# Causal attention scored with keys on partitions: row maxima from a rough first pass, no transposes of probabilities

## What is computed

```python
qkv = xn @ W_qkv                                  # 128 -> 2048 + 1024 + 1024
bias = slope[h] * (pos_k - pos_q)
scores = where(causal, q @ k.T / sqrt(64) + bias, -inf)
s = (softmax(scores) @ v).reshape(B, S, 2048) @ W_out
h = gelu(xn @ w1[e] + b1[e]); y = h @ w2[e] + b2[e]   # per expert e
ffn = sum over the 2 best experts of softmax weight * y
out = x + s * silu(ffn)
```

## Time and profile before

| | |
|---|---|
| Runs | 1374.01, 1370.53, 1371.32 us |
| Span of the profiled execution, first to last instruction | 1341.2 us |
| Profiled execution's own time | not listed; the median run is 30.1 us over the span |
| PE busy | 1257.6 us (94%) |
| DVE busy | 1237.7 us (92%) |
| ACT busy | 1082.2 us (81%) |
| POOL busy | 845.9 us (63%) |
| Mean granted TensorE clock | 0.984 of full speed |

### The profile page before, as it was taken

How to read it: one execution, slowest core, us unless ns; L and a number is a source line. 1 busy time by engine, 2 the same in 40 slices (tenths; PEclk the granted TensorE clock), 3 DMA queues, 4 the chain that set the end, 5 groups by cost and what they waited for, 6 DMA issues and landing times.

```text
span 1341.2 us, 56170 instructions
## 1 busy us (share of the span) xinstructions
PE 1257.6 (94%) x17434; PEld 1072.9 (80%) x17435; DVE 1237.7 (92%) x3788; ACT 1082.2 (81%) x2175; POOL 845.9 (63%) x993
## 2 busy tenths in 40 slices
PE   2599999999999999998999899999999999999993
PEld 1387888888888888886888678888888888888882
DVE  8798999999999999996888799999999999999996
ACT  1488998899889888885666688888888888888883
POOL 6277777777777777772000177777777777767774
PEclk9699999999999999999999999999999999999997
DMA  8132333323333333331222222222222222222222
GB/s 314 38 76 68 78 78 75 74 72 78 76 76 75 78 78 78 78 76 31 84 81 81 79 70 70 70 67 65 68 67 68 70 70 70 65 65 69 67 71 63
DMA packets 96213, 103.28 MB, mean 77 GB/s; under 512 B 17170, under 2 KB 76594, under 8 KB 95540
## 3 DMA queue, kind: packets, MB, share of 16 engines
q1 hardware_dynamic: 92084, 94.46, 27.5%
q0 software_dynamic: 4096, 8.40, 2.2%
HBM read 18.91 MB, written 16.78 MB: 27 GB/s over the span
## 4 chain that ended last, share of the span: by engine, by line
PE 89%; DVE 5%; issue 3%; ACT 1%; POOL 1%; DMA 1%; SPq 0%; ACTq 0%; DVEq 0%; POOLq 0%
PE ps L643 20%; PE ps L634 10%; PE ps L635 10%; PE ps L567 9%; PE ps L569 9%; PE ps L568 9%; PE ps L665 6%; PE ps L666 5%; PE ps L667 5%; PE ps L676 4%; PE ps L733 1%; DVE mix L945 1%; POOL h L547 1%; DMA X<-in_L_attn_inputs 1%; ACT stage L850 1%
## 5 line engine op out<-in xcount | busy, mean ns | idle before, releaser
L547 POOL TENSOR_TENSOR h<-stage 128x512 f16<-128x512 f32 x640 | 663.4, 1045 | 193.8 <-ACT stage L265 106.7
L850 ACT ACTIVATE stage<-stage,nmax 128x256 f32<-128x256 f32 (+3 forms) x1024 | 530.1, 564 | 17.4 <-DVE nmax L998 11.7
L998 DVE CUSTOM_DVE_ANT_0 stage<-ps,relpos,nslope_now 128x256 f32<-128x256 f32 (+3 forms) x1024 | 522.5, 543 | 12.8 <-PE ps L635 8.3
L643 PE MATMUL ps<-ident,stage 128*128 128x128 f32 x2560 | 389.8, 275 | 4.4 <-ACT stage L850 4.3
L265 ACT COPY stage<-ps 128x512 f32<-128x512 f32 x512 | 299.6, 586 | 89.4 <-PE ps L643 82.4
L643 PEld LDWEIGHTS ps<-ident,stage 128*128 128x128 f32 x2560 | 300.4, 141 | 63.8 <-ACT stage L850 19.5
L635 PE MATMUL ps<-k_st,q_st 128*128 128x256 f16 (+3 forms) x1024 | 299.5, 300 | 0.0
L634 PE MATMUL ps<-k_st,q_st 128*128 128x256 f16 (+3 forms) x1024 | 272.3, 299 | 12.8 <-DVE nmax L998 6.4
L665 PE MATMUL ps<-v_sp,stage 128*128 128x65 f16 x2560 | 265.6, 194 | 0.9 <-POOL h L547 0.9
L666 PE MATMUL ps<-v_sp,stage 128*128 128x64 f16 x2560 | 265.8, 193 | 0.0
L667 PE MATMUL ps<-v_sp,h 128*128 128x65 f16 x2560 | 264.7, 192 | 0.0
(11 more groups left out here) (170 smaller groups left out, 2604.2 us busy)
## 6 DMA issues: line engine op xcount, KB each, us to landing
q_st<-q_raw SPq DMA_DIRECT2D x512, 64.0 KB
k_st<-k_raw SPq DMA_DIRECT2D x256, 128.0 KB, 2.4
xg<-slot_x SPq DMA_DIRECT2D x40, 128.0 KB, 2.0
slot_y<-y_sb SPq DMA_DIRECT2D x40, 128.0 KB, 1.7
slot_x<-att SPq DMA_DIRECT2D x2, 2048.0 KB, 13.3
wx_raw<-in_L_ffn_w SPq DMA_DIRECT2D x64, 64.0 KB, 1.9
X<-in_L_attn_inputs SPq DMA_DIRECT2D x4, 512.0 KB, 5.7
stage<-in_L_attn_W_qkv SPq DMA_DIRECT2D x2, 1024.0 KB, 6.9
```

The source lines that it names most:

```text
L547: pool.tensor_tensor(t_lo[r], t_p[r], upper(t_p[r]), ALU.subtract).then_inc(s[f"lo{u % NG}"], 1)
L643: mm = pe.transpose(T_ps[u % 2][:, b * P:(b + 1) * P], prob[u % 2][:, b * P:(b + 1) * P], ident[:, :])
L850: e = act.activation(prob[u % 2][:, c0:c0 + w], neg_s[u % 2][:, c0:c0 + w], ACT.Exp, bias=nmax[:, u % 2, k:k + 1], scale=-1.0)
L998: ins = dve.tensor_tensor_reduce(neg_s[u % 2][:, c0:c0 + w], S_ps[u % 2][:, c0:c0 + w], relpos[:, SEQ - w:SEQ], nslope_now[:, sl, h:h + 1] ...
```

## The change

**Scores are computed transposed.** Keys stand on partitions, and queries in the free dimension. `GROUPS` is now cut by key tile kt (128 keys, the (4-kt)·128 queries that see them), again eight pieces in five groups. Exp then yields probabilities that already have keys on partitions, so T and X are gone, with `ON_ACT`, `neg_s`, `prob` and the two transposing banks.

**Bias and shift enter through the contraction.** `k_st` and `q_st` have two planes. Plane 0 is 128 rows deep (hi and lo of q against hi of k, twice). Plane 1 is 67 rows deep (`EXTRA`): hi of q against lo of k, the key position (row 64), and the shift of each query (row 65 holds c/1024 against 1024), with a last row for the query tile. A third matmul of 128 columns per piece (`ident16` against `maskT`) adds the causal mask to the diagonal block. Exp reads PSUM directly, with the head's slope as scale.

**Row maxima come from a rough pass.** M (`rough`): for each slot and head, hi of q (64 rows deep) against hi of k, queries on partitions, in three rounds per slot (`ROUNDS`) over two PSUM banks, one per head; head 0 uses partitions 0 to 63, head 1 64 to 127. B (`peaks`, DVE) replaces R: the same custom instruction with `kmask` in place of `relpos`, max in place of min, its full output thrown away (`junk`). C (`turn_shifts`, PE) transposes the 8 columns of maxima of a slot; ACT (`shifts`) makes 16-bit rows of them, and two small DMAs on SP (`place_shifts`) put them in row 65 of `q_st`. M and B of a body run one window ahead of its scores.

**The rest.** N handles both heads of a slot in one reciprocal and one product (two per body in place of four). The copies of the slopes (L1010) are gone. K and Q of slot 0 run two windows ahead; `k_st` and `v_sp` have two buffers, so the loop body is written out twice (`UNROLL`). The index copies on POOL (I) stand apart from the indirect DMAs (D) that need them. `go_ahead` starts each half with K, Q and V of its first body; six windows of a half are straight code ahead of the loop (two of them entering) and three behind it. POOL fills the constant rows once at the start.

```diff
-GROUPS = [[(0, 3, 0)], [(0, 0, 0), (0, 2, 128)], [(0, 1, 0), (1, 1, 256)], [(1, 3, 0)],
-          [(1, 0, 0), (1, 2, 128)]]
+GROUPS = [[(0, 0, 0)], [(0, 1, 0), (0, 3, 384)], [(0, 2, 0), (1, 2, 256)], [(1, 0, 0)],
+          [(1, 1, 0), (1, 3, 384)]]
+ROUNDS = [[(3, 0)], [(0, 0), (2, 128)], [(1, 0)]]
...
-        ("S0", 0), ("T9", -1), ("A0", -1), ("S1", 0), ("P5", -1), ("P7", -1), ("P6", -1),
+        ("S1", 0), ("C1", 0), ("P8", -1), ("P9", -1), ("S2", 0), ("M0", 1), ("A0", -1), ("S3", 0), ("A1", -1),
...
+            def rough(n, par, j):
+                sl, r = divmod(j, NR)
+                need(pe, f"qh{sl}", n + 1)
+                need(pe, f"kst{sl}", (n + 1) * 32)
+                if r == 0:
+                    need(pe, f"crow{1 - sl}", n + sl)
+                else:
+                    need(pe, f"peak{j - 1}", n + 1)
...
+                for i, c0 in ROUNDS[r]:
+                    w = (i + 1) * P
+                    for h in range(2):
+                        head = slice(DH * h, DH * h + DH)
+                        mm = pe.matmul(M_ps[h][:, c0:c0 + w], q_raw[sl][head, 0, i * P:(i + 1) * P],
+                                       k_st[par][sl][head, 0, 0:w], start=True, stop=True)
+                mm.then_inc(s[f"rough{j}"], 1)
+            def turn_shifts(n, _, sl):
+                for r in range(NR):
+                    need(pe, f"peak{sl * NR + r}", n + 1)
+                pe.transpose(M_ps[0][:, 0:P], mx[sl][:, :], ident[:, :]).then_inc(s[f"turnc{sl}"], 1)
...
-                group_done(pe, "shifted", n, u - 2)
...
+                need(pe, f"cst{sl}", (n + 1) * 32)
+                group_done(pe, "exp", n, u - 2)
...
+                for h, kt, c0 in GROUPS[u % NG]:
+                    d = S_ps[u % 2][:, c0:c0 + (QT - kt) * P]
+                    at, seen = slice(kt * P, (kt + 1) * P), slice(kt * P, SEQ)
+                    pe.matmul(d, k_st[par][sl][:, 0, at], q_st[sl][h][:, 0, seen], start=True, stop=False)
+                    pe.matmul(d, k_st[par][sl][0:EXTRA, 1, at], q_st[sl][h][0:EXTRA, 1, seen],
+                              start=False, stop=False)
+                    mm = pe.matmul(d[:, 0:P], ident16[:, :], maskT[:, :], start=False, stop=True)
...
-            def turn(n, u):
-                group_done(pe, "exp", n, u)
-                group_done(pe, "out", n, u - 2)
-                for b in range(4):
-                    mm = pe.transpose(T_ps[u % 2][:, b * P:(b + 1) * P],
-                                      prob[u % 2][:, b * P:(b + 1) * P], ident[:, :])
-                mm.then_inc(s[f"turned{u % NG}"], 1)
...
+            def shifts(n, _, sl):
+                act.wait_ge(s[f"turnc{sl}"], n + 1)
+                need(act, f"cst{sl}", n * 32)
+                act.activation(c16[sl][:, :], M_ps[0][0:2 * QT, 0:P], ACT.Copy, scale=-1.0 / 1024)\
+                   .then_inc(s[f"crow{sl}"], 1)
...
+                parts = [(0, 0, 256), (1, 256, 512)] if r == 2 else [(GROUPS[r][0][0], 0, 512)]
+                for h, c0, c1 in parts:
+                    e = act.activation(t_p[r][:, c0:c1], S_ps[u % 2][:, c0:c1], ACT.Exp,
+                                       scale=slope[:, bass.ds(pair_index(n) * 2 * SLOTS + sl * 2 + h, 1)])
...
+                for h in range(2):
+                    for i, c0 in ROUNDS[r]:
+                        w = (i + 1) * P
+                        ins = dve.tensor_tensor_reduce(
+                            junk[h][:, c0:c0 + w], M_ps[h][:, c0:c0 + w], kmask[:, SEQ - w:SEQ], 1.0, -3e38,
+                            ALU.add, ALU.max, mx[sl][:, h * QT + i:h * QT + i + 1])
...
+                for h in range(2):
+                    sp.dma_start(q_st[sl][h][POS + 1:POS + 2, 1, :], c16[sl][QT * h:QT * h + QT, :])\
+                      .then_inc(s[f"cst{sl}"], 16)
```

More of the change, by code:

```diff
@@ L233, in build @@
         s = {n: sem("s_" + n) for n in names}
-        for step in ("scored", "shifted", "exp", "turned", "out", "lo", "valued"):
+        for step in ("scored", "exp", "lo", "valued"):
             for u in range(NG):
                 s[f"{step}{u}"] = sem(f"s_{step}{u}")
+        for step in ("rough", "peak"):
+            for j in range(SLOTS * NR):
+                s[f"{step}{j}"] = sem(f"s_{step}{j}")
         block = ctx.enter_context(nc.Block())
@@ L253, in group_done, with slot_scored @@
             need(eng, f"{step}{u % NG}", n * SLOTS + u // NG + 1)
[L255 to L265 removed]
+        def slot_scored(eng, n, sl):
+            group_done(eng, "scored", n, sl * NG + NG - 1)
@@ L275, in enter_bodies, with go_ahead @@
+        def go_ahead(engine_name, tasks, lo, hi):
+            bodies_of_half[:] = lo, hi
+            for name in AHEAD[engine_name]:
+                tasks[name[0]](lo, lo % UNROLL, int(name[1:]))
         def enter_bodies(engine_name, tasks, lo, hi):
             bodies_of_half[:] = lo, hi
-            one_window(engine_name, tasks, lo - 1, lo, hi)
+            for w in (lo - 2, lo - 1):
+                one_window(engine_name, tasks, w, lo, hi, w)
         def run_bodies(eng, engine_name, tasks, lo, hi):
-            start = max(lo + 1, 2)
+            start, end = lo + 2 * UNROLL, hi - UNROLL
@@ L284, in run_bodies @@
             for w in range(lo, start):
-                one_window(engine_name, tasks, w, lo, hi)
-            with eng.Fori(start, hi - 1) as w_:
-                one_window(engine_name, tasks, w_, lo, hi)
-            for w in (hi - 1, hi):
-                one_window(engine_name, tasks, w, lo, hi)
+                one_window(engine_name, tasks, w, lo, hi, w)
+            with eng.Fori(start // UNROLL, end // UNROLL) as i_:
+                for c in range(UNROLL):
+                    one_window(engine_name, tasks, i_ * UNROLL + c, lo, hi, c)
@@ L292, in build @@
+            for w in range(end, hi + 1):
+                one_window(engine_name, tasks, w, lo, hi, w)
         stage_of = [stage[:, i, :] for i in range(NSTG)]
@@ new lines, in values @@
+                with_one = slice(V_HI - 1 + sl * (DH + 1), V_HI - 1 + (sl + 1) * (DH + 1))
+                lo = slice(V_LO + sl * DH, V_LO + (sl + 1) * DH)
+                for h, kt, c0 in GROUPS[r]:
+                    opens = r == (0, 2)[h]
+                    closes = (r, kt) == ((2, 2), (4, 3))[h]
+                    v = v_sp[par][:, kt, :]
+                    for i in range(kt, QT):
+                        d = O_ps[h][:, i * (DH + 1):(i + 1) * (DH + 1)]
+                        c = slice(c0 + (i - kt) * P, c0 + (i - kt + 1) * P)
+                        p_hi = upper(t_p[r])[:, c]
+                        pe.matmul(d, p_hi, v[:, with_one], start=(opens and i == kt), stop=False,
+                                  skip_group_check=True)
+                        pe.matmul(d[:, OUT_COL[sl]:OUT_COL[sl] + DH], p_hi, v[:, lo], start=False, stop=False,
+                                  skip_group_check=True)
+                        mm = pe.matmul(d, t_lo[r][:, c], v[:, with_one], start=False,
+                                       stop=(closes and i == QT - 1), skip_group_check=True)
@@ L692, in project @@
                 mm.then_inc(s["op"], 1)
-            tasks = {"Q": queries, "K": keys, "V": vals, "S": scores, "T": turn, "P": values,
+            tasks = {"Q": queries, "K": keys, "V": vals, "M": rough, "C": turn_shifts, "S": scores, "P": values,
                      "A": turn_out, "O": project}
             pe.wait_ge(s["wloD"], 2)
-            enter_bodies("PE", tasks, 0, HALF)
+            go_ahead("PE", tasks, 0, HALF)
             pe.wait_ge(s["picked"], 1)
```

360 lines of the change are left out of this document (195 added, 165 removed), and 15 rows, old and new, of the table ORDER.

## The result

The change took **1541.3 us** (median of 4 runs, 1536.4 to 1547.8) beside 1372.2 us for the kernel before (4 runs, 1370.5 to 1374.0): a ratio of 1.123, 95% interval 1.119 to 1.126. It is slower by 169 us, where 79 us less were predicted, and lies outside the range. The profiled execution took 1536.4 us, with a span of 1534.7.

What follows compares the result with a forecast made beforehand. PE was taken to bound attention: a body falls from 17.24 to 15.7 us, saving 98.6 us over 64 bodies, less 20 outside the steady state; 1371.3 - 78.6 = 1293 us, range 1245 to 1365.

Steps and rivals of the forecast that it cites:

- The moved DMAs: SP's queue: two new transfers placing the shifts, 4 small ones per body, taken as covered and priced at nothing.
- row changes: PE going from 128 rows to 64 and back, 12 times per body at 0.05 us: 0.60 us, bounds nothing and 1.98.
- Rival 3: PE's array empties at every change of rows, heads one after the other: 18.13 us per body, 1448 us; chance 0.12.
- Rival 2: Ping-pong: rough rounds on PE and their DVE reader wait for each other; 16.5 us per body, 1344 us; chance 0.20.
- Rival 1: Row changes on PE cost nothing: 15.1 us per body, 1254 us; chance 0.18.
- PE's sum: PE's work per body: 17.24 - 4.35 + 0.88 + 0.22 + 1.08 + 0.60 = 15.67 us.
- The other engines: Per body DVE 13.9 us, ACT about 10.5, POOL 12.6, all below PE's 15.7.
- Start-up: Outside the steady state, at the start of each half: +10 us per half, +20 in all, bounds 8 and 35.
- The base: Profiled span of 1341.2 us as start; the 30.1 us around it, up to the median run, stay.
- PE waiting at scores for the DMA of shifts (my uncosted chain): Listed sign of being wrong: PE stands at the scores until the shifts' transfer is done; no size given.
- PE at 97% or more: Listed sign of being right: PE's busy share in mid-attention.
- A sum into `att` every 15.5 to 16 us: Listed sign of being right: the once-per-body instruction repeats at this distance, for a body of 15.7 us.

Runs made afterwards that it cites:

- e11: The change with the first expert product on ACT and POOL's later index copy, SP's queue order left as in the change: 1541.4 us, ratio 1.124.
- e12: The kernel of e6 (SP order, expert product and index copy all moved) run again on another chip: 1339.3 us, ratio 0.975.
- e1: The change with one task moved in SP's queue, slot 1's queries ahead of its shifts: 1352.7 us, ratio 1.008.
- e5: e1 with the first expert product moved from DVE to ACT: 1324.5 us, ratio 0.986.
- e6: e1 with the first expert product on ACT and POOL's second index copy behind the first indirect DMA: 1324.1 us, ratio 0.986.
- e13: The kernel of e12 with each rough matmul issued twice, on the same chip: 1407.6 us, ratio 1.024.
- e15: The kernel before, unchanged, traced on the chip of e12: 1373.9 us, ratio 1.000.
- e4: e1 with POOL's second index copy moved behind the first indirect DMA: 1357.9 us, ratio 1.012.

## Why the prediction was wrong

**The step that failed** is "The moved DMAs: ... I price it at nothing". The text named what would happen if the cover were gone ("all of SP's queue behind it ... would be late too, and PE would stand at group 0 or 5"), but looked at slot 0 only, where it put 5 us between the transpose of maxima and the scores, and the trace has 7.7. For slot 1 the order of SP's queue puts its queries behind its shifts. The chain from the transpose (308.05) to the landing (316.06) takes 8.0 us, and PE has 5.4 us of other work in between (308.05 to 316.10 less the 2.65 of waiting). The landing stood in the earlier trace rows; SP's issue times, 4.8 us of the chain with the shifts' and the weights', stood in no row and no term. The queue cost 202 us (e11 against e12), some 61 of them by the clock after the stops, which no step foresaw.

**It was not the only step.** With the queue alone mended (e1) the span is 1351.5 us, beside 1341.2 before and the 1262.6 predicted, so the change would still have gained nothing. Against the prediction the bodies of the first half are 25 us too long in all, those of the second 55, and the starts of the halves 10. The 25 are mostly the row changes; the second half adds the held expert product, worth 28 (e5). Both are taken up below.

**Rival 3** turned the sign in the forecast, but was not the cause. A change of rows costs 0.10 us, twice the 0.05 taken (1.21 us per body instead of 0.60) and less than its bound of 0.165; the heads run side by side, as taken. This is above the 0.065 us from which the rival was to be slower only if all else was as it assumed, one head after the other. The Trainium skill ("TensorEngine Tiling (Array Packing)", section Key Properties) says that a change of tiling mode drains the engine. The trace agrees in so far as each change costs time, 0.095 us ahead of the pair above and 0.115 behind it; whether the array empties in it no run shows. **Rival 2** (ping-pong) did not come in the steady state: PE is full in e6's mid-attention. Its sign, PE waiting for L1079, came only in e1's second half, behind the held product. **Rival 1** fell with the row changes.

**PE's sum**, with the queue mended: 17.24 - 4.35 + 0.93 (masks, 0.88 taken) + 0.25 (maxima, 0.22) + 1.08 (rough pairs; 1.05 by e13) + 1.21 (row changes, 0.60) = 16.36 us, and 16.68 measured in e6. The prediction's sum was 15.67. Of the 1.01 us missing, 0.61 is the row changes and 0.08 masks and maxima. Most of the last 0.32 can be found in e6's trace. Each of the four groups of the values' projection ends with a longer step, 0.113 us on average where before has 0.056; that is 0.23. And each 67-row matmul holds PE 3 to 4 ns longer than the 128-row one beside it, 0.06 in all. Such a step hides in the busy time, since a 128-column matmul is listed for 0.22 us:

```profile
308.84 0.22 PE L610 MATMUL ps<-wv_hi,xT_lo 128*128 x1
308.97 0.23 PE L608 MATMUL ps<-wv_hi,xT_hi 128*128 x1
```

Why the projection's steps are longer stays open.

**The other engines.** DVE came to 14.0 us per body in e6 (168.39 of 200 us at 16.68), where 13.9 was said; ACT to 10.8 (10.5 said) and POOL to 12.7 (12.6). What the sum of durations could not show is an instruction that grows with its place: F0 took 0.28 us in the change, where all ran late behind SP's chain, and 1.55 us once that was mended, and with DVE far from full (166.97 of 200 us in e1's second half) it cost 28 us, because PE's next round waits behind it.

**Start-up.** 20 us in all were taken, with bounds of 8 and 35. Measured are 17.7 + 16.2 = 33.9 us in the change and 16.2 + 11.6 = 27.8 in e12 (107.9 to the first sum, 181.4 across the expert stage): inside the bounds, and 8 to 14 us more than taken. The first exponential starts at 73.5 us, where before has 62.9.

**The base.** "What lies around it, 30.1 us up to the median run, stays" was wrong. Only 1.7 us lie around the span of e15 and of the change. With as much the first trace's 1341.2 us would be a run of 1343, the time that the kernel has on the chips of the faster rhythm, so the trace and the timed runs seem to come from different rhythms (the chip of the first trace is not recorded). The sum then started from a body of 17.24 us where the timed kernel had 17.35 and 18.17.

**The signals.** "PE waiting at scores for the DMA of shifts (my uncosted chain)" was the listed sign that came, with the queries behind the shifts in place of the shifts. Of the signs of being right, "pairs of rough matmuls starting a few ns apart" and "DVE under 92%" came; "PE at 97% or more" came only once the queue was mended. "A sum into `att` every 15.5 to 16 us" did not come even in the best version.

## What to carry to other kernels

When a change puts a transfer with a late condition into a queue that issues in order, list what stands behind it in that queue and add up the issue times (0.6 to 0.7 us each here) and the last landing against the first reader of each; one entry moved was worth 202 of 1541 us here (e11 against e12). A second queue is no free cure: on ACT the same two transfers cost 34 us by their issue time. And before a body time is taken from a profile, compare that execution's own time with the timed runs; 2% between them was another rhythm of the same program, and no overhead.

## What the hardware showed that was not expected

- **A DVE instruction held by POOL.** Instructions of 128x128 whose operands are all in SBUF took 1.55 us instead of 0.28 (L1138 in e1) and 1.18 instead of 0.40 (L1064 in e15), and ended 0.1 to 0.15 us behind POOL's. The Trainium skill ("SBUF — State Buffer", section "SBUF: two separate sides") has VectorE and GpSimd share one pair of ports as "an exclusive lock, not a bandwidth split", held for the whole instruction, taken by VectorE instructions with two SBUF inputs or in a two-port mode. The traces agree: the whole delay falls on one instruction, and PSUM readers beside POOL keep their time (in e1 L1079 of 512 columns takes 0.69 us on average with a POOL instruction beside it and 0.68 without). In one thing they go further: in e1 and e4 the product began inside POOL's first instruction and ended behind the second, so it was passed over once. Whether the product runs in a two-port mode no trace shows.
- **Chips that differ by rhythm.** The kernel before took 1342 us in two of the comparisons and 1372 to 1374 us in the three others, on other chips, with all its mean durations but one within 3% from 900 to 1100 us, so a ratio measured on one kind of chip does not hold on the other: 0.986 and 0.975 for the best version.
- **The clock after stops.** PE stops of 2.65 to 3.0 us, once per body, brought the granted clock of 300 to 500 us from 1.00 to 0.90 (0.89 in e11), and the steps behind a stop fell to those of the lower of its two levels, 1.2 GHz; stops of 1.0 to 1.7 us once per body in the second half of the change left it at 1.00 from 1100 to 1300 us.
